# In the second of two bitonic sorts, the key goes to its place by a copy and two predicated copies instead of by minimum and maximum

## The reference, cut to what matters

```python
def _L0_gnn_ref(h, e, src, dst, ...):
    z_src = z[src]
    ...
    a = z_src @ blk[0] + z_dst @ blk[K] + ex @ w_e
    ...
    m = jax.ops.segment_max(att, dst, num_segments=N)
    expv = jnp.exp(att - m[dst])
    denom = jax.ops.segment_sum(expv, dst, num_segments=N)
    ...
    return jax.ops.segment_sum(msg, dst, num_segments=N)
```

## Time and profile before

| what | value |
|---|---|
| median of the timed runs | 13628.68 us (13624.3 to 13629.43) |
| span of the profiled execution | 13681.3 us |
| first sort | until some 535 us of the span |
| second sort | 563.7 to 3095 us |
| VectorE, GpSimd, ScalarE busy in the whole span | 42%, 65%, 17% |

### The profile page before, as it was taken

How to read it: one execution, slowest core, us unless ns; L and a number is a source line. 1 busy time by engine, 2 the same in 40 slices (tenths; PEclk the granted TensorE clock), 3 DMA queues, 4 the chain that set the end, 5 groups by cost and what they waited for, 6 DMA issues and landing times. The chain is left out here.

```text
span 13681.3 us, 56503 instructions
## 1 busy us (share of the span) xinstructions
PE 2507.4 (18%) x11588; PEld 1958.1 (14%) x11588; DVE 5746.5 (42%) x14196; ACT 2306.2 (17%) x3572; POOL 8888.7 (65%) x8546
## 2 busy tenths in 40 slices
PE   0122322233000000000000002555555560000000
PEld 0121222222000000000000002444444440000000
DVE  8777777687222222321111112555555532222223
ACT  0122333230011111112121210111111121111111
POOL 0266767671777777667777776555555547777776
PEclk8555555555555555555555556777777765555555
DMA  4000000001111112111111111222222202111111
GB/s 168 17 13 13 11 11 11 11 12 40 37 50 49 50 49 50 46 49 48 46 47 48 46 48 48 69 68 67 69 68 68 60 14 49 49 48 48 49 48 47
DMA packets 688745, 628.08 MB, mean 46 GB/s; under 512 B 453486, under 2 KB 511495, under 8 KB 687505
## 3 DMA queue, kind: packets, MB, share of 16 engines
q0 software_dynamic: 273056, 240.52, 9.9%
q1 hardware_dynamic: 413614, 372.84, 8.3%
q10 hardware_dynamic: 1728, 11.11, 0.2%
HBM read 319.01 MB, written 304.83 MB: 46 GB/s over the span
## 5 line engine op out<-in xcount | busy, mean ns | idle before, releaser
L1104 POOL DMA_INDIRECT l_rows<-table,l_sources x4704 | 4941.1, 1050 | 1613.6 <-issue 1570.4
L548 POOL DMA_INDIRECT e_rows<-in_rec,base x1568 | 1763.5, 1125 | 809.1 <-issue 461.6
L1104 POOL DMA_INDIRECT l_pair<-table,l_slab x1568 | 1496.9, 955 | 1029.7 <-issue 518.4
L1301 DVE TENSOR_TENSOR_SCAN l_totals<-l_factor,banks 128x510 f32<-128x510 f32 (+3 forms) x672 | 752.7, 1162 | 1899.1 <-ACT banks L1456 1898.2
L1232 DVE TENSOR_TENSOR l_score<-l_rows,base 128x14 f32<-128x14 f32 x224 | 43.1, 192 | 3214.6 <-DMA l_rows<-table,l_sources 3214.6
L1466 ACT COPY l_kept<-l_totals 128x476 f32<-128x476 f32 (+3 forms) x672 | 638.7, 966 | 3717.6 <-issue 2868.9
L1418 PE MATMUL banks<-ident,l_kept 128*65 128x128 f32 (+2 forms) x4 | 1.9, 463 | 6742.1 <-DVE junk L1350 4564.1
L1418 PEld LDWEIGHTS banks<-ident,l_kept 128*65 128x65 f32 (+2 forms) x4 | 0.7, 170 | 6743.4 <-DVE junk L1350 4564.7
L703 PE MATMUL banks<-Z 125*128 125x98 bf16 x3200 | 623.0, 366 | 1710.6 <-DVE Z L686 1524.6
L1408 PE MATMUL banks<-w_each,l_turned 128*128 128x288 f32 (+1 forms) x1344 | 709.0, 619 | 1136.6 <-ACT l_turned L1488 628.9
L407 ACT COPY area<-area 128x2048 f32<-128x2048 f32 x342 | 642.6, 1927 | 1509.7 <-DVE area L332 1253.6
(11 more groups left out here) (323 smaller groups left out, 5598.8 us busy)
## 6 DMA issues: line engine op xcount, KB each, us to landing
l_rows<-table,l_sources POOLq DMA_INDIRECT x4704
sums<-l_kept SPq DMA_DIRECT2D x112, 476.0 KB
sums<-l_kept SPq DMA_DIRECT2D x224, 231.0 KB
sums<-l_kept SPq DMA_DIRECT2D x112, 462.0 KB
seeds<-zeros SPq DMA_DIRECT2D x130, 392.0 KB
sums<-l_kept SPq DMA_DIRECT2D x112, 448.0 KB
l_pair<-seeds SPq DMA_DIRECT2D x224, 224.0 KB
e_rows<-in_rec,base POOLq DMA_INDIRECT x1568
```

The lines of the kernel that those rows point to most:

```text
L548: GP.indirect_dma_start(e_rows[:, u, g, :], None, A["rec16"], bass.IndirectOffsetOnAxis(e_ids[:, s * G16 + g:s * G16 + g + 1], 0)).then_in ...
L1104: GP.indirect_dma_start(pair[:, u, g, 0:D] if gated else rows[:, u, g, :], None, table[l], bass.IndirectOffsetOnAxis(at, 0)).then_inc(rows ...
L1301: V.tensor_tensor_scan(flat(totals[:, s % 2, h, 0:n, :]), flat(factor[:, s % 2, 0:n, :]), flat(fresh[s % 2][h][:, 0:n, :]), 0.0, ALU.mult, ...
```

## The change

In every stage of the second sort that is not flipped, minimum and maximum of the key are dropped. ScalarE copies the key from `key[side]` to `key[1-side]` (one copy of 2048 words) ahead of its two feature copies. VectorE, after the mask, overwrites the swapped words of the key with two `copy_predicated` of 1024 words each, taken from the other half, and then does the features as before. The first sort and the flipped stages keep minimum and maximum. `copies_until` counts ScalarE's copies, three in a stage and two in a flipped one.

```diff
+        def copies_until(n):
+            return sum(2 + (not (in_rows(e["j"]) and e["j"] == e["k"] - 1)) for e in PLAN[:n])
...
+                by_mask = loads and not flipped
...
-                for (lo, hi, up), (to_lo, to_hi, _) in zip(ins, outs):
+                for (lo, hi, up), (to_lo, to_hi, _) in zip(ins, outs if not by_mask else []):
                     for to, op in ((to_lo, ALU.min if up else ALU.max), (to_hi, ALU.max if up else ALU.min)):
...
                 if loads:
-                    ins_.then_inc(s["swap"], 1)
+                    low = 1 << address_bit(j)
+                    (ins_m if by_mask else ins_).then_inc(s["swap"], 1)
                     dve.wait_ge(s["swap"], n + 1)
-                    low = 1 << address_bit(j)
+                    if by_mask:
+                        dve.wait_ge(s["copied"], copies_until(n) + 1)
+                        key_was, key_to = (key[i].rearrange("p (x j l) -> p x j l", j=2, l=low) for i in (side, 1 - side))
+                        for i in range(2):
+                            V.copy_predicated(key_to[:, :, i, :], swap.rearrange("p (x l) -> p x l", l=low),
+                                              key_was[:, :, 1 - i, :])
...
                     for i in range(2):
-                        dve.wait_ge(s["copied"], 2 * n + i + 1)
+                        dve.wait_ge(s["copied"], copies_until(n + 1) - 1 + i)
                         ins_ = V.copy_predicated(to[i], m, was[1 - i])
...
+                    if not (in_rows(j) and j == k - 1):
+                        AC.copy(key[1 - e["side"]][:], key[e["side"]][:]).then_inc(s["copied"], 1)
                     was, to = halves(loads[e["load_side"]], j), halves(loads[1 - e["load_side"]], j)
                     for i in range(2):
                         AC.copy(to[i], was[i]).then_inc(s["copied"], 1)
```

More of the change, by code:

```diff
@@ L314, in sort_vector @@
                         if flipped:
-                            V.scalar_tensor_tensor(m, hi, -1.0, lo, ALU.mult, ALU.is_lt if up else ALU.is_gt)
+                            ins_m = V.scalar_tensor_tensor(m, hi, -1.0, lo, ALU.mult, ALU.is_lt if up else ALU.is_gt)
                         else:
-                            V.tensor_tensor(m, lo, hi, ALU.is_gt if up else ALU.is_lt)
-                for (lo, hi, up), (to_lo, to_hi, _) in zip(ins, outs):
+                            ins_m = V.tensor_tensor(m, lo, hi, ALU.is_gt if up else ALU.is_lt)
+                for (lo, hi, up), (to_lo, to_hi, _) in zip(ins, outs if not by_mask else []):
                     for to, op in ((to_lo, ALU.min if up else ALU.max), (to_hi, ALU.max if up else ALU.min)):
```

## The result

The changed kernel takes 13713.9 us (median of four runs, 13703.0 to 13722.6), the kernel before, measured beside it, 13629.1 (13624.3 to 13638.8). The ratio is 1.0061, 95% interval 1.0047 to 1.0075: **slower by 0.6%**, 85 us. The prediction was 13600 us, range 13560 to 13670; the time lies outside.

What follows compares the result with a forecast made beforehand. For long stretches of the second sort GpSimd's gathers set the pace, VectorE being held by late increments. Terms +35, +6, -64, -6 and 0 gave -29 us: 13600 us from the timed median, range 13560 to 13670.

Steps and rivals of the forecast that it cites:

- VectorE's bill: Second sort: VectorE's own time change, 0.2 us gained per two-way stage, nothing in ordinary one-way stages, 2.2 lost in 17 slow ones.
- The slow strides: One-way stages at compare distance 2 and 1: two key copies take 4.5 us instead of 2.39; 16 x 2.2 = +35 us.
- The ordinary pair: Other one-way stages: two key copies take 2.3 to 2.4 us, against 2.39 for minimum and maximum, so no change.
- ScalarE's copy: Behind the seven moves back: VectorE waits 0.8 us for ScalarE's copy of the key, +6 us in all.
- GpSimd's relief: One-way stages: gathers of 1.97 us beside minimum and maximum fall to 0.94; -64 us in row stages, -6 in column stages.
- The wider relief in two-way stages: By the skill's page, relief would reach the 70 two-way stages, 0.3 us each, making the time 20 us lower; not in the forecast.
- rival 2: Late increments spread to one-way stages; one more catching up per block costs 7.4 us: 13650, two each 13700; 13%.
- GpSimd's wait behind the move back: Sign that the forecast is right: this wait in the second sort is near 31.5 us instead of 28.6.
- Rival 1: Second sort follows VectorE after all, relief lost in each k's nine row stages, up to +41 us: 13655 to 13670; 15%.
- rival 4: Gain and loss cancel within 27 us, part of the relief going into longer standing at the next catching up: 13628; 15%.
- Rival 3: Key copies aren't slow at compare distance 1 and 2: -35 us more, 13565; 15%.
- The -3 us of two-way stages (I had -14): VectorE gains 0.2 us in each of 70 two-way stages, 14 us, counted as 0 because GpSimd paces those stretches.

Runs made afterwards that it cites:

- paused_after_again: Changed kernel with GpSimd's gathers paused around the second sort's moves, against the kernel before without pauses (13667.0 us), on the slower chip: 13580.6 us, ratio 0.9943.
- second execution: The changed kernel run again, unaltered, against the kernel before (13667.0 us) on the slower kind of chip: 13742.0 us, ratio 1.0057.
- two_way_only: Key moved by the mask in two-way stages alone, one-way stages keeping minimum and maximum, against the kernel before (13633.2 us): 13628.8 us, ratio 0.9999.
- one_way_only: Key moved by the mask in one-way stages alone, the others as in the kernel before (13633.2 us): 13732.6 us, ratio 1.0070.
- paused_before_again: Kernel before with GpSimd's gathers paused around the second sort's moves, against the same without pauses (13667.0 us), on the slower chip: 13584.4 us, ratio 0.9940.

## Why the prediction was wrong

*What bounds the kernel.* That VectorE is held until GpSimd has caught up, by increments that come late, was right, and right on this kind of chip only. Its place was too narrow. I read late increments in two-way stages and at moves back, and took the moves into columns as lasting 19 to 33 us "though GpSimd is busy throughout", for a time of their own. They are 11.9 to 12.9 us in `paused_after_again`, where GpSimd is paused; the rest was lag already.

*VectorE's bill.* The slow strides were right, and a little dearer than the 4.5 us forecast: a pair of key copies takes 4.80 us in the first stage behind a move back. The ordinary pair was mis-sized a little: 2.55 us in the mean instead of 2.3 to 2.4, over 78 stages some 15 us that the sum had as nothing. ScalarE's copy was right (5.7 us in 8 waits, against 6). The sum +35 + 6 stood against +57 in one-way stages.

*GpSimd's relief*, **the term of -64 and -6 us, is the step that failed**, twice. The gathers of 1.97 us are gone as predicted, 91 to 2. But 32 others are held for 3.7 to 5.9 us, through two or four histogram instructions and the mask in one chain, and the sum of held time fell by 8 us (35 in the second execution) instead of 90. And the sum took it that the points where GpSimd catches up would stay. They moved: in the stretch from 1806 to 1880 us GpSimd began 48 gathers instead of 44,

```profile
1806.00:1880.00 74.00, 59.56 (x48) 0.50 0.10 14
```

the increments fell behind at the next move into columns, the moves took 50 us in the mean instead of 29 (43 in the second execution), and GpSimd stood once more, 11 to 17 us a block longer in all.

*The Trainium skill's rule* (SBUF — State Buffer, Who interferes with whom) that the second to start blocks fully fits the 3.79 us gather; that a chain of VectorE instructions counts as one for it is what the row adds. The wider relief in two-way stages that I weighed by that page didn't come: `two_way_only` was no quicker, and on the quicker chip slower.

*The rivals.* What happened is nearest to rival 2, late increments spread, with one more catching up in each block (13% for 13650 to 13700): not mainly ahead of histogram steps in one-way stages, as I had it, but at the move behind them, and at 11 to 17 us each instead of 7.4. Its sign, new waits of VectorE in one-way stages, is missing in the first trace (all 97.7 us lie in two-way stages) and there in the second, 44 us in four places. GpSimd's wait behind the move back did speak against the forecast in the first trace: 24.3 us, less than the 28.6 of before, where 31.5 was forecast. Rival 1 (VectorE paces the sort) holds on the other kind of chip, and rival 4 (gain and loss cancel) is what the times showed there. Rival 3 was wrong. The -3 us of two-way stages (I had -14) are hidden as predicted.

What stays open: where the 26 us of the loss lie that the two traces don't place in the sort; why gathers are now held through histogram and mask in one piece; why `one_way_only` lost more than the whole change (99 against 85 us, with intervals that overlap), and how much of the lag a better placed pause would still take, since VectorE stood 205 us at moves back and 208 us at histogram steps even with pauses.

## What to carry to other kernels

- Price an edit between the points at which two engines meet, but ask first whether it moves those points. Here gathers relieved by 1 us each came closer together, and GpSimd met VectorE once more in every block from k = 13 on.
- A wait that is long while the engine named has been idle can be an increment that comes late, as it was here (the semaphore's increments are in the trace). Look for it at every handover of that pair of engines, not only where it was seen first, and measure what the handover takes with the third engine silent (11.9 us here, instead of 30 to 50). Pausing the third engine for some 9 us around each was worth 0.6%, more than any change of instructions here.
- Where two chains end at one junction with 49 us between them, a shift of work from one to the other gives nothing beyond that: 52 us more in the one and 57 less in the other left the time as it was.

## What the runs showed that I had not expected

- Two kinds of chip: the kernel before takes 13629 to 13667 us on one and 11926 to 11936 on the other. On the first, TensorE's increments are late while gathers run (each carry of a move 3 to 10 us, waits put down to "remote"), on the second they are not, with the same gathers 0.30 us apart. TensorE's granted clock doesn't explain it: 0.566 and 0.569 in the mean. The late increments aren't the whole of the 1700 us either: the sort takes 2531 us on the one and 2030 on the other (with pauses), and most of the difference lies behind it, where no run looked for its cause.
- A predicated copy of 1024 words with its mask in PSUM takes 1.22 to 2.54 us, 1.33 in the middle; at distance 1 and 2 a pair takes 4.8 us, while minimum and maximum at these strides kept their 2.39 us a pair.
- It is enough to silence GpSimd's gathers, and with them their DMA traffic, for the increments of a move to be on time: ScalarE's 164 copies more stand in `paused_after_again` too, and cost nothing there. In `paused_before_again` the same pause brought the moves into columns only to 16 to 20 us each, from 29 in the mean. Whether it is GpSimd's issuing or the traffic, no run separates.
